# A gated delta-rule recurrence: side work of every engine in smaller pieces at other leaves, decay products on GpSimd, selector matmuls over row halves

## The chip, the core and the metric

The kernel is one launch on one core of a Trainium2 chip. The metric is the device time in microseconds of the whole launch, over several runs.

## The reference

An attention layer with a gated delta-rule state (2048 tokens, 16 heads of width 128) and after it a mixture-of-experts layer. The change is in the scan:

```python
def step(S, t):
    q_t, k_t, v_t, a_t, b_t = t
    y = jnp.einsum('bhvk,bhk->bhv', S, k_t)
    err = y - v_t
    S = a_t[..., None] * S - (b_t[..., None] * err)[..., None] * k_t[:, :, None, :]
    o = jnp.einsum('bhvk,bhk->bhv', S, q_t)
    return (S, o)
```

The outputs o are then normed over the head width, scaled by a gate and multiplied by Wo.

## The kernel before, in words

Three stages follow each other: projections and convolutions (tiles named A_), the recurrence (`recurrence`, tiles named B_), the experts (C_). The change is inside `recurrence`.

The recurrence takes 32 **chunks** of 64 tokens in order. A chunk has 16 **leaves** of 4 tokens, `j` from 0 to 15. A leaf is a chain over three engines. VectorE multiplies the coefficients with what came from the left (L1068), adds them up (L1071) and decays the result (L1073). TensorE transposes it into PSUM (L1576), ScalarE copies it to `WL`, and TensorE multiplies it with grams of keys and queries into `psM` (L1586 and L1588 for an even leaf, L1595 and L1603 for an odd one); the next leaf's L1068 reads that. `merge_of(j)` gives the size of the merge: even leaves merge 4 tokens, leaves 1, 5, 9, 13 merge 8, leaves 3 and 11 merge 16, leaf 7 merges 32. In the last two kinds the left side is first compacted into `WC` by ScalarE (`left_compact`). On the way the ends of the parts are scaled: by VectorE for even leaves (`scale_leaf`, L1031, and `scale_leaf_w`, L1036), by GpSimd for odd ones (`scale_right`, L822 and L830; `scale_left`, L840). After leaf 15 comes the **turn**: transposes of the whole W, the update of the state `ST` (L1541, L1018), and the next chunk's product of state with keys and queries (`contact`, L1449), copied by ScalarE.

All else is **side work**, and each engine has it written out by hand between leaves. For TensorE it is a table, `leaf_jobs(g, j)`, whose jobs are issued after leaf `j`'s merge: `qk` and `kk` (one row of queries or keys spread over all partitions by a selector, L1472), `own` and `gram` (grams, L1459 and L1495), `ktok` (transposed keys), `decay`, `oc`, `var`, `dev`, `rstd` (centering and norm of the outputs, L1517 is `var`), `wo` (output projection, L1533, in odd chunks only), `update`. Each job takes the next of five PSUM banks in turn and waits until the bank's last job has been read (`open_bank`). VectorE takes the banks: `y_terms` (L991) for `qk`, `row_pairs` for `kk`, `mask_own` and `mask_gram`, `decay_state` (L1012), `norm`. It also solves the leaves' small systems in eight steps (`leaf_solution`, L954) and makes the next chunk's decay products in three instructions (`decays`, L916, L919, L921). GpSimd's order is the list at the end of its block, where `past(g, j)` waits for VectorE to pass leaf `j`.

## Time and profile before

| what | value |
|---|---|
| runs | median 3173.81 us of 3 (3172.24 to 3183.9) |
| the profiled execution | 3174.62 us, span 3172.8 us |
| TensorE matmul, weight load | 2838.1 us (89%), 2012.0 us (63%) |
| VectorE | 2322.8 us (73%) |
| ScalarE | 1605.5 us (51%) |
| GpSimd | 1317.6 us (42%) |
| first and last L1068 of the recurrence | 642.2 us, 2781.9 us |

The two L1068 times bound the recurrence. The profile's slices show TensorE at 8 to 9 tenths and VectorE at 7 to 8 tenths over the whole of it. A matmul's record overlaps the next one's, so TensorE's busy time is more than its work.

### The profile page before, as it was taken

Reading aid. Unit: us, or ns where it says so; the run is one execution under the profiler, and the core shown is the slowest. Engines: PE = TensorE matmul, PEld = TensorE weight load, DVE = VectorE, ACT = ScalarE, POOL = GpSimd, SP = SyncE. Lnnn points to the kernel's source line nnn. Section 1 sums busy time; section 2 is a strip of 40 time slices with the busy share of each in tenths; the row PEclk is TensorE's granted clock in tenths of the full one; section 3 lists DMA queues with packets and bytes.
Section 4 is the critical chain, followed back from the end, with each engine's and each line's share of the span. In section 5 each row is a group of like instructions: output and inputs, shape, how many; then the busy total and the mean of one; then the engine's idle time right before and its main releaser. Section 6 shows DMA issues by size and latency. Waiting matters only on the chain. (4 is left out here: it accounts for less than half of the span.)

```text
span 3172.8 us, 48588 instructions
## 1 busy us (share of the span) xinstructions
PE 2838.1 (89%) x14144; PEld 2012.0 (63%) x14144; DVE 2322.8 (73%) x4837; ACT 1605.5 (51%) x3516; POOL 1317.6 (42%) x1574
## 2 busy tenths in 40 slices
PE   7999999678898898988989898898888989869999
PEld 3555555366676776666766676776767767645555
DVE  6777777578888778887787878788887788724332
ACT  6666666445555555554554555555555555421111
POOL 3666767624443444443443434444334444310000
PEclk9999999889999999999999999999999999979999
DMA  3655565631222322222323222322223222034220
GB/s 133 242 202 231 234 241 202 225 60 34 54 42 41 60 51 54 43 41 42 69 41 55 41 42 43 67 46 51 42 41 65 46 54 42 8 105 89 55 44 14
DMA packets 449884, 261.23 MB, mean 82 GB/s; under 512 B 402672, under 2 KB 414672, under 8 KB 447472
## 3 DMA queue, kind: packets, MB, share of 16 engines
q1 hardware_dynamic: 449664, 258.51, 31.5%
q8 instruction: 113, 1.85, 0.3%
q14 instruction: 107, 0.88, 0.1%
HBM read 153.42 MB, written 105.05 MB: 81 GB/s over the span
## 5 line engine op out<-in xcount | busy, mean ns | idle before, releaser
L265 DVE SCALAR_TENSOR_TENSOR A_acc<-A_psY,A_w,A_acc 128x410 f32<-128x410 f32 (+1 forms) x720 | 419.2, 637 | 151.6 <-ACT A_acc L334 151.6
L1155 ACT ACTIVATE B_WL<-B_psT 64x128 f32<-64x128 f32 (+3 forms) x480 | 148.6, 310 | 512.4 <-PE B_psT L1576 512.4
L840 POOL TENSOR_TENSOR B_WT<-B_WT,B_G 128x128 f32<-128x128 f32 (+2 forms) x224 | 183.0, 817 | 513.0 <-PE B_psT L1576 493.3
L405 PE MATMUL A_psY<-A_xT,A_w 128*128 128x413 f32 (+1 forms) x960 | 347.2, 510 | 9.1 <-PE A_psAG L411 7.7
L192 POOL TENSOR_TENSOR A_outs<-A_outs,A_acc 128x410 f32<-128x410 f32 (+1 forms) x240 | 229.7, 987 | 215.5 <-ACT A_outs L342 215.5
L1068 DVE TENSOR_TENSOR B_NC<-B_NC,B_psM 128x256 f32<-128x256 f32 x480 | 199.1, 415 | 143.9 <-PE B_psM L1603 101.8
L405 PEld LDWEIGHTS A_psY<-A_xT,A_w 128*128 128x128 f32 x960 | 180.2, 189 | 165.5 <-issue 164.2
L822 POOL TENSOR_TENSOR B_PQ<-B_PQ,B_G 128x256 f32<-128x256 f32 x128 | 125.8, 983 | 368.3 <-DVE B_WT L1036 368.3
L1071 DVE TENSOR_REDUCE B_W<-B_NC 128x64 f32<-128x320 f32 x512 | 248.7, 486 | 17.6
L1603 PE MATMUL B_psM<-B_BD,B_WL 128*128 128x128 f32 x1536 | 237.6, 296 | 12.6
L334 ACT ACTIVATE A_acc<-A_psY,A_w 128x410 f32<-128x410 f32 (+1 forms) x240 | 166.2, 692 | 162.9 <-PE A_psY L405 161.2
L1603 PEld LDWEIGHTS B_psM<-B_BD,B_WL 128*128 128x128 f32 x1536 | 195.9, 197 | 81.0 <-ACT B_WL L1155 80.3
L1155 ACT ACTIVATE B_PQ<-B_psM 128x64 f32<-128x64 f32 (+2 forms) x480 | 124.5, 259 | 220.8 <-DVE B_NC L1068 215.7
L411 PE MATMUL A_psAG<-A_xT,A_w 128*128 128x410 f32 (+1 forms) x640 | 233.1, 506 | 0.0
L830 POOL TENSOR_TENSOR B_PQ<-B_PQ,B_G 128x256 f32<-128x256 f32 (+1 forms) x192 | 174.9, 924 | 42.7 <-DVE B_WT L1036 42.7
L411 PEld LDWEIGHTS A_psAG<-A_xT,A_w 128*128 128x128 f32 x640 | 121.0, 189 | 99.6 <-issue 99.6
L954 DVE TENSOR_TENSOR B_NC<-B_NC,B_TMP 128x384 f32<-128x384 f32 (+1 forms) x192 | 164.5, 857 | 4.4
L1472 PE MATMUL B_ring<-B_QS,B_source 128*128 128x128 f32 (+1 forms) x896 | 158.7, 323 | 0.0
L793 POOL TENSOR_TENSOR B_SQ<-B_PQ,B_E 128x256 f32<-128x256 f32 x128 | 125.5, 981 | 71.1 <-DVE B_WT L1073 67.4
L1896 ACT ACTIVATE C_act_g<-C_psG 128x512 f32<-128x512 f32 (+1 forms) x56 | 33.4, 597 | 228.5 <-PE C_psU L1951 228.5
L1459 PE MATMUL B_ring<-B_KQ,B_KL 128*128 128x256 f32 x512 | 126.1, 390 | 25.6 <-DMA B_KQ<-scr 25.6
L1588 PE MATMUL B_psM<-B_OWN,B_WL 64*128 64x128 f32 x512 | 120.6, 315 | 20.0 <-ACT B_WL L1155 20.0
(197 smaller groups left out, 6703.5 us busy)
## 6 DMA issues: line engine op xcount, KB each, us to landing
B_KQ<-scr SPq DMA_DIRECT2D x96, 512.0 KB, 6.8
scr<-A_outs SPq DMA_DIRECT2D x48, 615.0 KB, 3.5
scr<-A_outag SPq DMA_DIRECT2D x32, 615.0 KB, 5.2
scr<-A_outs SPq DMA_DIRECT2D x48, 409.0 KB, 2.5
A_xc<-nbeta SPq DMA_DIRECT2D x16, 1024.0 KB, 5.9
B_A<-scr SPq DMA_DIRECT2D x32, 512.0 KB, 5.0
B_C<-scr SPq DMA_DIRECT2D x32, 512.0 KB, 5.9
B_G<-scr SPq DMA_DIRECT2D x32, 512.0 KB, 4.6
```

The costliest lines, as they stand in the source:

```text
L192: nc.gpsimd.tensor_tensor(o, o, acc[:, p, n % 2, 0:t1 - t0], ALU.mult).then_inc(silu[p].sem, 1)
L265: nc.vector.scalar_tensor_tensor(a, y, w[:, s, col:col + 1], a, ALU.mult, ALU.add)\
L334: nc.scalar.activation(acc[:, p, n % 2, 0:t1 - t0], psY[p][:, y0:y0 + t1 - t0], ACT.Identity, scale=w[:, s, col + HALO:col + HALO + 1], bi ...
L405: last = nc.tensor.matmul(psY[p][:, y0:y0 + HALO + t1 - t0], wp[:, p, kt, :], xT[:, kt, t0:t1 + HALO], start=kt == 0, stop=kt == KT - 1)
L411: last = nc.tensor.matmul(psAG[p][:, 0:t1 - t0], wp[:, A_ + p, kt, :], xT[:, kt, HALO + t0:HALO + t1], start=kt == 0, stop=kt == KT - 1)
L830: tt(x, x, gl.to_broadcast([128, H, n]), ALU.mult).then_inc(psc.sem, 1)
L840: tt(dst, dst, gr, ALU.mult).then_inc(wsc.sem, 1)
L954: tt(out, in0, in1, op).then_inc(ncs.sem, 1)
L1068: tt(eq[:, :, :, 1:5], eq[:, :, :, 1:5], left.unsqueeze(2).to_broadcast([128, H, R, R]), ALU.mult)\
L1071: nc.vector.tensor_reduce(W[:, :, lf], eq, AXIS.X, ALU.add).then_inc(ws.sem, 1)
L1155: copy = lambda out, in_: nc.scalar.activation(out, in_, ACT.Copy)
L1603: last = mm(psM[:, 512 * q + rs * i:512 * q + rs * (i + 1)], WL[0:rs, 128 * i:128 * (i + 1)], BD[0:rs, bank, col + rs * part:col + rs * (p ...
```

## The change

- The three decay products of the next chunk leave VectorE (`decays`) and become six products of one row each on GpSimd (`row_decays`), two behind leaf 2 and one each at leaves 6, 7 and twice at 9.
- The selector jobs `kk` and `qk` go over row halves: each of the two leaves of a pair has its own 64 rows and its own bank, and the matmuls alternate between the halves. `qk` is three jobs, not five, and `y_terms` reads two banks at a time. `update` alternates in the same way.
- A second table, `short_jobs`, puts TensorE's jobs between a leaf's transpose and its merge. Most jobs stand at other leaves; `wo` is cut in two halves.
- VectorE's side work moves with them; the eight solution steps are placed one by one, and the last of the next chunk's stands after the state update.
- In leaves 3, 7 and 11 VectorE writes its result straight into the compact array `WC`; ScalarE copies it from there to `WT` afterwards.
- In even leaves after the first, the product with `WL` comes before the one with the identity.
- Banks are given to the job by who had them longest ago, with two neighbouring ones for `kk` and `qk`. ScalarE's side work is regrouped.

```diff
+def short_jobs(g, j):
+    first, last, out, wo = g == 0, g + 1 == NCH, g > 0, g % 2 and g >= 3
+    jobs = {
+        2: [("own", 1, 1)],
+        3: [("ktok", 0)],
+        8: ([("own", 0, 0)] if not last else []),
+        10: [("gram", 5)],
+        14: ([("wo", 1)] if wo else []),
+    }
...
-            1: [("own", 1, 0), ("own", 1, 1)],
-            2: [("ktok", 0), ("gram", 1)] + (out and [("qk", 2)] or []),
-            3: out and [("qk", 3), ("qk", 4)],
-            4: [("kk", 1, 0), ("kk", 1, 1), ("gram", 4)],
-            5: out and [("oc", 0)],
-            6: out and [("oc", 1)],
-            7: out and [("oc_rest", 1)],
-            8: (g % 2 and [("ktok", 1)] or []) + ([] if last else [("own", 0, 0), ("own", 0, 1)]),
-            9: [("gram", 5), ("decay", 0), ("decay", 1)],
-            10: [] if last else [("kk", 0, 0), ("kk", 0, 1)],
-            11: out and [("var", 0)],
-            12: (out and [("dev", 0)] or []) + ([] if last else [("gram", 0)]) + (wo and [("wo", 0)] or []),
-            13: [("decay", 2), ("decay", 3)],
-            14: (wo and [("wo", 1)] or []) + (out and [("rstd", 0), ("rstd", 1)] or [])
-                + (not g % 2 and [("ktok", 1)] or [])}
-    return jobs.get(j) or []
+    jobs = {
+        -1: [("gram", 2), ("gram", 3)],
+        0: ([("qk", 0, 0), ("qk", 0, 1)] if out else []),
+        1: [("own", 1, 0)],
+        2: [("gram", 1)],
+        3: ([("qk", 1, 0), ("qk", 1, 1), ("qk", 2, 0), ("qk", 2, 1)] if out else []),
+        4: [("kk", 1, 0), ("kk", 1, 1), ("gram", 4)],
+        5: ([("oc", 0)] if out else []),
+        6: ([("oc", 1)] if out else []),
+        7: [("decay", 0)] + ([("oc_rest", 1)] if out else []),
+        8: ([("own", 0, 1)] if not last else []),
+        9: [("decay", 1)],
+        10: ([("kk", 0, 0), ("kk", 0, 1)] if not last else []) + ([("var", 0)] if out else []),
+        11: ([("wo", 0)] if wo else []),
+        12: ([("gram", 0)] if not last else []) + ([("dev", 0)] if out else []) + ([("wo_rest", 0)] if wo else []),
+        13: [("decay", 2), ("decay", 3)],
+        14: [("ktok", 1)] + ([("rstd", 0)] if out else []) + ([("wo_rest", 1)] if wo else []) + ([("rstd", 1)] if out else []),
+    }
+    return jobs.get(j, [])
...
-OUT_ROWS = [((0, 0, 2),), ((1, 1, 2),), ((2, 2, 2),), ((3, 3, 1), (0, 2, 1)), ((1, 3, 1), (0, 3, 1))]
+OUT_ROWS = [((0, 0, 2), (1, 1, 2)), ((2, 2, 2), (3, 3, 1), (0, 2, 1)), ((1, 3, 1), (0, 3, 1))]
+KEY_ROWS = ((0, 1, 3), (1, 2, 2), (2, 3, 1))
...
+            def row_decays(g, *parts):
+                a, e = by_leaf_row(A[:, g % 2]), E[:, g % 2]
+                products = ((RR_, a[:, 1], a[:, 2]), (B_, e[:, RR_], a[:, 3]), (F_ + 1, a[:, 0], a[:, 1]),
+                            (B_ + 1, a[:, 2], a[:, 3]), (F_ + 2, e[:, F_ + 1], a[:, 2]), (F_ + 3, e[:, F_ + 2], a[:, 3]))
+                for k in parts:
+                    row, x, y = products[k]
+                    if k == 0:
+                        loaded(pool, "A", g)
+                        wait(pool, nc0, 2 * g - 3, 5)
+                    else:
+                        wait(pool, dec, g, {1: 1, 4: 3, 5: 5}.get(k, 0))
+                    tt(e[:, row], x, y, ALU.mult).then_inc(dec.sem, 1)
...
+                if more:
+                    row_decays(g + 1, 0)
+                    row_decays(g + 1, 1)
...
                 past(g, 4)
                 scale_right(g, 5)
-                gates(3)
+                scale_left(g, 3)
                 past(g, 5)
-                queries(3)
+                if g:
+                    decayed_q(g - 1, 3)
+                if g >= 2:
+                    gate(g - 2, 3)
+                scale_right(g, 7, (0,))
                 scale_left(g, 5)
-                scale_right(g, 7, (0,))
+                scale_left(g, 7)
                 past(g, 6)
                 scale_right(g, 7, (1,))
+                if more:
+                    row_decays(g + 1, 2)
                 past(g, 7)
-                scale_left(g, 7)
+                if more:
+                    row_decays(g + 1, 3)
                 past(g, 8)
                 scale_right(g, 9)
                 past(g, 9)
+                if more:
+                    row_decays(g + 1, 4)
                 scale_left(g, 9)
+                if more:
+                    row_decays(g + 1, 5)
+                past(g, 11)
                 scale_right(g, 11)
-                past(g, 11)
-                scale_left(g, 11)
                 past(g, 12)
                 scale_right(g, 13)
-                past(g, 13)
+                scale_left(g, 11)
+                past(g, 14)
                 scale_left(g, 13)
...
-                wait(dve, awm, o, (4, 5, 3, 6, 6)[n])
-                ps = take_bank(dve, o + 1, "qk", n)
-                x = WX[:, 2 * n:2 * n + 2]
-                tt(x, ps[:].rearrange("p (n c) -> p n c", n=2), x, ALU.mult).then_inc(yv.sem, 1)
+                wait(dve, awm, o, (5, 6, 6)[n])
+                m = 4 if n < 2 else 2
+                ps = take_two_banks(dve, o + 1, "qk", n)[:, :, 0:m * HJ2]
+                x = WX[:, 4 * n:4 * n + m].rearrange("p k (l x) -> p l k x", l=2)
+                tt(x, ps.rearrange("p l (k x) -> p l k x", k=m), x, ALU.mult).then_inc(yv.sem, 1)
...
-                    tt(WT[:, j] if j % 2 else WR[:], W[:, :, lf], E[:, g % 2, B_:B_ + R, :, j].rearrange("p r h -> p h r"), ALU.mult).then_inc(wt.sem, 1)
+                    p, n, _ = merge_of(j)
+                    if j < JM and p >= 2:
+                        to = WC[:, 0:H * n].rearrange("p (h t) -> p h t", h=H)[:, :, n - R:n]
+                    else:
+                        to = WT[:, j] if j % 2 else WR[:]
+                    tt(to, W[:, :, lf], E[:, g % 2, B_:B_ + R, :, j].rearrange("p r h -> p h r"), ALU.mult).then_inc(wt.sem, 1)
...
+                    elif j == 8:
+                        if more:
+                            mask_own(g + 1, 0, 0)
                     elif j == 9:
                         if more:
-                            decays(g + 1, (1,))
-                            mask_own(g + 1, 0, 0)
                             mask_own(g + 1, 0, 1)
                     elif j == 10:
+                        decay_state(g, 0)
                         mask_gram(g, 5)
-                        decay_state(g, 0)
+                    elif j == 11:
                         decay_state(g, 1)
-                    elif j == 11 and more:
-                        row_pairs(nxt)
-                        leaf_solution(nxt, 1, 2)
-                    elif j == 12 and more:
-                        leaf_solution(nxt, 2, 4)
+                        if more:
+                            row_pairs(nxt)
+                            leaf_solution(nxt, 1)
+                    elif j == 12:
+                        if more:
+                            leaf_solution(nxt, 2)
...
-                        if p >= 2:
-                            wait(act, wt, g, j + 1)
-                            left_compact(g, j, (j,))
                         wait(act, tps, g, j + 1)
                         wait(act, mps, g, 2 * j)
                         w_ = 128 << max(p - 1, 0)
                         rows_ = 64 if p == 0 else 128
                         copy(WL[0:rows_, 0:w_], psT[0:rows_, 0:w_]).then_inc(wl.sem, 1)
+                        if p >= 2:
+                            wait(act, wt, g, j + 1)
+                            copy(WT[:, j], WC[:, 0:H * n].rearrange("p (h t) -> p h t", h=H)[:, :, n - R:n]).then_inc(wc.sem, 1)
                     if j == 13:
...
+            def row_scalars(g, kind, n):
+                if kind == "qk":
+                    rows, runs, width = QS[:, (g - 1) % 2].rearrange("p t h n -> p t (h n)"), OUT_ROWS[n], HJ2
+                else:
+                    rows, runs, width = KS[:], KEY_ROWS, HJ2 // 2
+                filled = [open_bank(pe, g, kind, n, leaf)[1] for leaf in range(2)]
+                if kind == "qk":
+                    wait(pe, qs, 2 * (g - 1) + 1, 1)
+                else:
+                    wait(pe, ks, 2 * g + (1 if n else 2), 1)
+                ps = two_banks(g, kind, n)
+                at = 0
+                for k, (r, t0, m) in enumerate(runs):
+                    for leaf in range(2):
+                        p = slice(64 * leaf, 64 * leaf + 64)
+                        c = R * leaf + r
+                        last = mm(ps[:, leaf, at * width:(at + m) * width].rearrange("p (t x) -> p t x", t=m),
+                                  source[p, c:c + 1].to_broadcast([64, 128]),
+                                  rows[p, R * leaf + t0:R * leaf + t0 + m], start=True, stop=True)
+                        if k == len(runs) - 1:
+                            last.then_inc(filled[leaf], 1)
...
+            def updates(g, half):
+                opened = [open_bank(pe, g, "update", 2 * half + r) for r in range(2)]
+                wait(pe, wtok, g, half + 1)
+                wait(pe, ktok, g, 2)
+                for m in range(4):
+                    i = 4 * half + m
+                    for r, (ps, filled) in enumerate(opened):
+                        p = slice(64 * r, 64 * r + 64)
+                        last = mm(ps[:, 128 * m:128 * (m + 1)], KTOK[p, i, :], WTOK[p, i, :], start=True, stop=True)
+                        if m == 3:
+                            last.then_inc(filled, 1)
...
                             wait(pe, ow, g, 2 if j < 8 else 4)
-                            wait(pe, psc0, g, pair_number(j) + 1)
-                            mm(psM[:, 0:2 * rs], ident[:], pair(g)[:, :, :, r0:r0 + n], start=True, stop=False)
-                            wait(pe, wl, g, j + 1)
-                            mm(psM[:, 0:2 * rs], WL[0:rs, 0:128], OWN[0:rs, j // 2, :, :, R:2 * R],
-                               start=False, stop=True).then_inc(mps.sem, 2)
+                            if j:
+                                wait(pe, wl, g, j + 1)
+                                mm(psM[:, 0:2 * rs], WL[0:rs, 0:128], OWN[0:rs, j // 2, :, :, R:2 * R], start=True, stop=False)
+                                wait(pe, psc0, g, pair_number(j) + 1)
+                                mm(psM[:, 0:2 * rs], ident[:], pair(g)[:, :, :, r0:r0 + n],```

VectorE's queue at leaves 8 to 10 of an even chunk (L1068 begins a leaf). Before:

```order
L1068 TENSOR_TENSOR B_NC<-B_NC,B_psM 128x16x4x4
L1071 TENSOR_REDUCE B_W<-B_NC 128x16x4
L1073 TENSOR_TENSOR B_WR<-B_W,B_E 128x64
L1045 TENSOR_TENSOR B_PQ<-B_PQ,B_psM 128x16x32
L1031 TENSOR_TENSOR B_PQ<-B_PQ,B_E 128x32x4
L1036 TENSOR_TENSOR B_WT<-B_WR,B_E 128x64
L916 TENSOR_TENSOR B_E<-B_A 128x3x256
L1068 TENSOR_TENSOR B_NC<-B_NC,B_psM 128x16x4x4
L1071 TENSOR_REDUCE B_W<-B_NC 128x16x4
L1073 TENSOR_TENSOR B_WT<-B_W,B_E 128x64
L919 TENSOR_TENSOR B_E<-B_E,B_A 128x2x256
L921 TENSOR_TENSOR B_E<-B_E,B_A 128x256
```

The same place in the changed kernel (L1137, L1140 and L1147 are the leaf's three, L1052 is `mask_own`):

```order
L1137 TENSOR_TENSOR B_NC<-B_NC,B_psM 128x16x4x4
L1140 TENSOR_REDUCE B_W<-B_NC 128x16x4
L1147 TENSOR_TENSOR B_WR<-B_W,B_E 128x64
L1114 TENSOR_TENSOR B_PQ<-B_PQ,B_psM 128x16x32
L1100 TENSOR_TENSOR B_PQ<-B_PQ,B_E 128x32x4
L1105 TENSOR_TENSOR B_WT<-B_WR,B_E 128x64
L1052 TENSOR_TENSOR B_OWN<-B_ring,B_causal 128x512
L1137 TENSOR_TENSOR B_NC<-B_NC,B_psM 128x16x4x4
L1140 TENSOR_REDUCE B_W<-B_NC 128x16x4
L1147 TENSOR_TENSOR B_WT<-B_W,B_E 128x64
L1052 TENSOR_TENSOR B_OWN<-B_ring,B_causal 128x512
```

The decays are gone, and one mask stands at each leaf where both stood behind leaf 9.

TensorE's queue from the merge of leaf 10 to the transposes of leaf 11, before:

```order
L1588 MATMUL B_psM<-B_OWN,B_WL 128x128
L1472 MATMUL B_ring<-B_KS,B_source 128x3x64 x2
L1472 MATMUL B_ring<-B_KS,B_source 128x2x64 x2
L1472 MATMUL B_ring<-B_KS,B_source 128x64 x2
L1576 MATMUL B_psT<-ident,B_WE 128x128 x2
```

And changed (L1590 is `gram`, L1733 and L1735 the merge, L1649 `kk`, L1612 `var`, L1723 the transposes):

```order
L1590 MATMUL B_ring<-B_KQ,B_KC 128x256 x2
L1733 MATMUL B_psM<-B_OWN,B_WL 128x128
L1735 MATMUL B_psM<-B_PQ,ident 128x128
L1649 MATMUL B_ring<-B_KS,B_source 128x192 x2
L1649 MATMUL B_ring<-B_KS,B_source 128x128 x2
L1649 MATMUL B_ring<-B_KS,B_source 128x64 x2
L1612 MATMUL B_ring<-B_SQ,B_avgcol 8x128 x8
L1723 MATMUL B_psT<-ident,B_WE 128x128 x2
```

`var` has moved from behind leaf 11 to behind leaf 10, and `gram` 5 in front of leaf 10's merge.

## Rows read from the trace of the kernel before

**Rows 1.** Windows, three chunks: engines' busy us, clock; even, odd, even.

```profile
core 0: us, PE busy (x) PEld busy (x) DVE busy (x) ACT busy (x) POOL busy (x), PEclk, DMA share, GB/s
1989.79:2054.51 64.72, 56.84 (x345) 43.45 (x344) 54.52 (x120) 36.12 (x85) 28.81 (x35) 1.00 0.28 49
2054.51:2123.29 68.78, 63.04 (x377) 49.62 (x376) 55.08 (x121) 36.40 (x86) 28.61 (x35) 1.00 0.26 49
1045.00:1112.00 67.00, 59.30 (x344) 45.55 (x343) 54.97 (x120) 36.05 (x85) 28.41 (x35) 0.95 0.27 48
```

**Rows 2.** Windows, even chunk: leaves 1, 2, 4, 6 and 7, 8 to 15.

```profile
1992.33:1995.22 2.89, 2.75 (x15) 2.30 (x16) 2.48 (x5) 1.86 (x9) 2.61 (x5) 1.00 0.03 6
1995.22:1998.49 3.27, 3.27 (x20) 2.74 (x19) 2.91 (x8) 1.97 (x5) 1.80 (x3) 1.00 0.01 5
2002.02:2005.27 3.25, 3.07 (x26) 2.74 (x24) 3.07 (x8) 1.86 (x7) 1.34 (x3) 1.00 0.00 0
2008.84:2018.71 9.87, 8.62 (x40) 5.14 (x39) 9.49 (x18) 4.59 (x10) 3.82 (x3) 1.00 0.36 60
2018.71:2022.47 3.76, 3.43 (x14) 1.99 (x13) 3.59 (x8) 2.19 (x4) 1.26 (x1) 1.00 0.00 0
2022.47:2026.72 4.25, 4.25 (x26) 3.40 (x24) 4.14 (x8) 1.09 (x3) 3.02 (x4) 1.00 0.00 0
2026.72:2030.39 3.67, 2.19 (x13) 1.60 (x12) 3.50 (x10) 3.32 (x8) 0.00 (x0) 1.00 0.00 0
2030.39:2033.65 3.26, 2.50 (x19) 1.97 (x18) 2.79 (x9) 1.77 (x7) 0.99 (x1) 1.00 0.00 0
2033.65:2037.24 3.59, 3.36 (x27) 2.45 (x26) 3.42 (x8) 1.40 (x4) 1.05 (x2) 1.00 0.02 5
2037.24:2040.38 3.14, 2.85 (x17) 2.16 (x18) 3.04 (x8) 1.73 (x4) 0.71 (x1) 1.00 0.00 0
2040.38:2044.00 3.62, 2.38 (x17) 1.72 (x15) 3.41 (x10) 1.32 (x4) 0.00 (x0) 1.00 0.01 2
2044.00:2054.51 10.51, 9.13 (x84) 8.36 (x82) 6.03 (x12) 6.58 (x10) 6.83 (x10) 1.00 0.86 152
```

**Rows 3.** Windows, odd chunk: leaf 13, and leaf 15 with the turn.

```profile
2101.99:2107.46 5.47, 5.33 (x27) 4.57 (x28) 3.03 (x8) 1.58 (x4) 0.46 (x1) 1.00 0.00 0
...
2111.10:2123.29 12.19, 11.89 (x99) 11.07 (x98) 6.54 (x13) 6.10 (x9) 6.83 (x10) 1.00 0.79 144
```

**Rows 4.** Groups of instructions, VectorE, whole launch: busy us, mean ns.

```profile
L991 DVE TENSOR_TENSOR B_WX<-B_ring,B_WX 128x512 f32<-128x512 f32 x160 | 107.3, 687 | 8.1 <-PE B_ring L1472 6.4
L916 DVE TENSOR_TENSOR B_E<-B_A 128x768 f32<-128x768 f32 x32 | 50.3, 1573 | 1.7 <-ACT B_E L1155 1.5 <-issue 0.2
L919 DVE TENSOR_TENSOR B_E<-B_E,B_A 128x512 f32<-128x512 f32 x32 | 34.7, 1085 | 0.3
L921 DVE TENSOR_TENSOR B_E<-B_E,B_A 128x256 f32<-128x256 f32 x32 | 24.5, 766 | 1.1
```

**Rows 5.** Timeline, TensorE: start us, us, line, shape, passes.

```profile
1976.74 3.72 PE L1533 MATMUL B_ring<-B_wo,B_OG 128*128 128x256 f32 x16
...
2002.27 1.95 PE L1472 MATMUL B_ring<-B_QS,B_source 128*128 128x128 f32 x16
...
2029.50 1.75 PE L1472 MATMUL B_ring<-B_KS,B_source 128*128 128x192 f32 x12
...
2033.99 1.91 PE L1517 MATMUL B_ring<-B_SQ,B_avgcol 128*8 128x128 f32 x16
...
2047.23 2.79 PE L1541 MATMUL B_ring<-B_WTOK,B_KTOK 64*128 64x128 f32 x32 [0.30 <-issue]
```

**Rows 6.** Timeline: a solution step beside GpSimd's work and without it.

```profile
2010.89 1.54 POOL L830 TENSOR_TENSOR B_PQ<-B_PQ,B_G 128x512 f32<-128x512 f32 x1 [1.33 <-DVE B_WT L1036]
2011.49 1.42 DVE L954 TENSOR_TENSOR B_NC<-B_X,B_NC 128x256 f32<-128x256 f32 x1
...
2035.67 0.61 DVE L954 TENSOR_TENSOR B_NC<-B_X,B_NC 128x256 f32<-128x256 f32 x1
```

390 lines of the change are left out of this document (223 added, 167 removed).

## The prediction, made blind

> **What bounds the kernel now.** I read the busy slices first: the recurrence fills two thirds of the span, with no engine full and the same pattern throughout, and the change is in it alone. So the next view is the table of windows, one chunk of 64 tokens each [rows 1]: an even chunk takes 64.72 us, an odd one 68.78. In the even one VectorE is busy 54.52 us and TensorE 56.84, and the reader should see that neither share is a bound by itself: TensorE's record overlaps itself, and each leaf of four tokens is a chain (VectorE solves the leaf, TensorE transposes it, ScalarE copies it, TensorE merges it, VectorE takes the result). A leaf's time is the longer of two things: that chain, with the side work in front of it on TensorE, or the work in VectorE's own queue. The windows by leaf [rows 2] tell which. Leaves 6 and 7 together: VectorE 9.49 of 9.87 us; leaf 8: 3.59 of 3.76; leaf 9: 4.14 of 4.25; leaf 10: 3.50 of 3.67; leaf 14 of the even chunk: 3.41 of 3.62. Those are VectorE's. Leaf 1 (2.48 of 2.89) and leaf 13 of the odd chunk (3.03 of 5.47) [rows 3] are TensorE's. At the chunk's turn (leaf 15) it is a serial chain: 6.03 of 10.51.
>
> **What the operations cost.** The three decay products cost VectorE 1573, 1085 and 766 ns, 3.42 us a chunk [rows 4]. They go to GpSimd as six products of 256 elements. VectorE's y terms are five of 687 ns [rows 4]; three with the same elements in all keep most of that, a 512-element one standing every 0.62 us, so I take 0.15 us off. On TensorE an fp32 matmul is two passes. 16 passes of 128 columns over all 128 rows take 1.91 to 1.95 us, 0.12 each; the state update's 32 passes of the same width on 64 rows, first one half of the rows, then the other, take 2.79 us, 0.09 each [rows 5]. So a row half starts before the other has ended. For alternating halves the bounds are 0.12 (no gain) and 0.06 (full overlap); I take 0.065, as the row shows overlap already where the halves only meet at a boundary. The selector job of the keys, 12 passes in 1.75 us [rows 5], becomes about 0.9, twice a chunk. The queries have 16 passes of 128 columns (1.95) and 12 twice as wide, about 4.4 us together, and go to 2.3.
>
> **Leaf by leaf**, in us a chunk, before from [rows 2, 3]:
> Leaf 1: the query job in front of its transpose shrinks from 1.7 to 0.9 us, so the transpose goes when VectorE is done (1.3 instead of 1.7 us into the leaf): −0.4.
> Leaf 2: half of the own-gram job now stands between transpose and merge, and the mask waits for it: +0.25.
> Leaf 4: it takes over 1.7 us of y terms where it had 1.3, and was at 3.07 of 3.25: with 0.2 us of gaps 3.85, +0.6.
> Leaves 6 and 7: GpSimd's scaling of the right part is moved out of leaf 6 and now follows the scaling of the left part in leaf 7. In leaf 6 it stood in VectorE's way: the solution step that begins at 2011.49 takes 1.42 us, and the same step takes 0.61 us at 2035.67 when GpSimd is still [rows 6]. The 0.8 us saved in leaf 6 is paid in leaf 7: −0.1.
> Leaf 8: loses the first decay product (1.57), gains a mask of 0.68 us, but waits for a job between transpose and merge behind decay 0 and the centered rest: 3.5, −0.25.
> Leaf 9: loses 1.85 us of decays and a mask; the chain of 3.0 us is left: −1.25.
> Leaf 10: loses one state decay (0.68) but has a gram between transpose and merge: 3.35, −0.3.
> Leaf 11: TensorE now has key selectors (0.9) and the variance job (16 passes, 1.91 [rows 5]) in front of the transpose, 2.8 us into the leaf instead of 1.6, and it was TensorE's leaf: +1.1.
> These eight sum to −0.35, in every chunk.
> Even chunks: leaf 12 without the variance job and with one solution step less, −0.65; leaf 13 has a solution step of 0.86 more on VectorE, +0.8; leaf 14 one less and its mask first, −0.55; leaf 15 as before. Together −0.4, so −0.75.
> Odd chunks: the output projection, 16 passes of 256 columns in 3.72 us [rows 5] in front of leaf 13, is halved there: 5.47 becomes 4.4, −1.1. Leaf 12 gets the first half, 0. Leaf 14 gets a half between transpose and merge, +0.4. The turn has 3.1 us instead of 3.7 in front of its transposes, −0.6. Together −1.3, so −1.65.
> Leaves 0, 3 and 5 I cost at nothing: the compaction that goes from leaf 3 is replaced by GpSimd's two decays beside it, and in leaf 5 ScalarE's copies of the key rows end when they did. If that cover is gone each is worth 0.3 us, either way. The last solution step after the state update lies under VectorE's wait for the contact copies (10.51 − 6.03 us idle in the turn [rows 2]).
>
> **What moves past what.** The decays wait in GpSimd's queue for nothing that is late: A is loaded a chunk ahead, and the first of them stands behind leaf 2. Behind them in that queue are the scalings for leaves 5, 9 and 11; each has over 1 us to spare, by GpSimd's 28.81 busy of 64.72 us [rows 1], which becomes about 34. ScalarE's leaf diagonals wait for the sixth product, which I place half a microsecond into leaf 10, and they start later. No DMA is added, and SP's queue sees the same semaphores. Key and query selectors need two neighbouring PSUM banks; the key job of leaf 4 waits 0.3 us for a y term's banks, under VectorE's 3.85 us. In even leaves after the first, the WL product now goes ahead of the identity product, so two matmuls follow the copy instead of one (about +0.2), where VectorE's scaling was late anyway: nothing.
>
> **The sum.** 16 × 0.75 + 15 × 1.65 = 37 us. The profiled execution took 3174.6 us (span 3172.8), the median of the runs is 3173.8, so the two agree: **3137 us**. Each leaf's term may be off by 0.3 us, which over a chunk is about 1 us, or 31 us in all: the forecast's own range is 3105 to 3168.
>
> **A rule on GpSimd.** The solution steps in [rows 6] show VectorE and GpSimd taking turns: one step of 0.61 us became 1.42. The Trainium skill (GPSIMD Engine Reference, section 8, Key points) says that GpSimd shares its SBUF interfaces with VectorE where VectorE's instruction has two SBUF inputs; by that rule, and the trace agrees, the decays could slow VectorE although they left its queue. That is the slower rival below.
> **A rule on row halves.** The pass of 64 rows costs less in [rows 5], with the update's two halves one behind the other. The Trainium skill (TensorEngine Tiling, Key Properties) says that a change of tiling mode drains TensorE. The change adds such switches round the selector jobs of leaves 3, 4 and 10; if each cost a pass and more, the gain of the halves would be gone.
>
> **The rivals.**
> *VectorE bounds all of it.* Then a chunk loses all of the 3.57 us that leave its queue: 31 × 3.57 = 111, **3063 us**. For it: 54.5 us busy in either kind of chunk [rows 1]. Against it: in odd leaf 13 and in leaf 11 it waits.
> *Slower by the shared port.* The six products on GpSimd each can hold a two-input step of VectorE by 0.8 us as in [rows 6]. My sum is −1.2 us a chunk, so it turns at 1.5 such holds; with three of the six it is +1.2 × 31, **3211 us**. For it: products 3 to 6 are queued behind leaves 6 to 9, the first of them behind two scalings that already collide. Against it: VectorE reads PSUM in most of its work there.
> *The halves don't overlap, or switching eats it.* Leaf 1 gives nothing, leaf 11 costs 0.75 more: +1.15 a chunk, **3173 us**, no change.
> *The clock.* A chunk in which the granted clock was 0.95 took 67.00 us against 64.72 [rows 1]. That window holds both levels, 2.4 and 1.2 GHz, while the other two chunks there stay at 1.00, and its work was the even chunk's. For it: TensorE gets less to do. If half of the chunks had that: +2.3 × 16, again **3173 us**.
>
> **How the numbers follow.** My forecast 0.47, VectorE's bound 0.20, no overlap 0.12, the port 0.11, the clock 0.10. A difference of 0.5% (16 us) is about what a measurement here can tell. Faster than 3158: 0.38 of the forecast's share, 0.20, and 0.06 of the milder halves of the others, 0.64. Within 0.5%: 0.08, and 0.10 from overlap and clock, 0.18. Slower: 0.18, of it 0.10 the port, the rest the bad ends of clock and overlap. The range reaches from the second case (3063, rounded down) to just short of the port's price: 3060 to 3200.
>
> **What would show it.** Right: leaf 9 near 3.0 us, leaf 4 near 3.9, leaf 11 near 4.3, odd leaf 13 near 4.4; selector passes starting in pairs; VectorE busy about 51 us a chunk. Wrong: solution steps of 1.4 us in more places than before (port), selector passes still 0.11 us apart (overlap), clock windows under 1.00 in most chunks, or leaf 11 near 3.3 (then I have misread what stands before its transpose).

## The result, and the profile after

The changed kernel took **3100.56 us** in the median (3098.51 to 3104.37 over 4 runs), the kernel before 3174.42 (3172.24 to 3183.9): ratio 0.9763, 95% interval [0.9747, 0.9779], so 74 us faster. Forecast were 3137 us, 37 us faster. The direction held, and the time lies in the whole range of 3060 to 3200 us, but 5 us outside the forecast's own of 3105 to 3168: the gain is twice the one that the sum gave. The profiled execution of the changed kernel took 3104.37 us (span 3102.6, mean granted clock 0.976; before 0.977).

Windows of one even and one odd chunk, as in [rows 1]:

```profile
core 0: us, PE busy (x) PEld busy (x) DVE busy (x) ACT busy (x) POOL busy (x), PEclk, DMA share, GB/s
1940.50:2003.46 62.96, 53.29 (x345) 38.96 (x344) 51.88 (x116) 36.26 (x85) 30.53 (x41) 1.00 0.28 52
2003.46:2069.57 66.11, 59.72 (x377) 44.65 (x376) 52.65 (x117) 36.56 (x86) 30.54 (x41) 1.00 0.26 50
```

The even chunk lost 1.76 us and the odd one 2.67. 16 × 1.76 + 15 × 2.67 = 68 us. In the two profiled executions the recurrence is 72 us shorter, and the other 4 are chunks with a lower clock. They are more now, but each costs less: of the 15 even chunks from 2 to 30, 9 have a stretch under 1.00 and take 0.7 to 2.0 us longer for it; before, 5 had one, for 2.3 to 2.5 us, and one odd chunk, for 3.3. VectorE is busy 51.88 us instead of 54.52, GpSimd 30.53 instead of 28.81.

The even chunk by leaf: leaves 1, 4 to 13 and 15 (leaf 7 begins at 1963.45). A leaf is counted from VectorE's first multiplication in it (L1137) to that of the next.

```profile
1943.05:1945.57 2.52, 2.02 (x15) 1.39 (x12) 2.31 (x5) 1.60 (x4) 2.52 (x5) 1.00 0.40 79
1952.56:1956.32 3.76, 3.31 (x33) 2.62 (x33) 3.59 (x9) 2.96 (x7) 1.36 (x2) 1.00 0.00 0
1956.32:1959.43 3.11, 2.97 (x24) 2.37 (x21) 2.54 (x8) 1.54 (x6) 1.80 (x3) 1.00 0.00 0
1959.43:1963.45 4.02, 3.57 (x13) 1.88 (x12) 3.85 (x11) 1.51 (x4) 1.30 (x2) 1.00 0.84 169
1963.45:1969.46 6.01, 5.79 (x32) 3.78 (x31) 5.80 (x9) 3.10 (x6) 3.06 (x3) 1.00 0.42 66
1969.46:1972.94 3.48, 3.45 (x14) 1.98 (x14) 2.89 (x7) 1.80 (x3) 1.74 (x3) 1.00 0.00 0
1972.94:1975.46 2.52, 2.02 (x11) 1.34 (x10) 1.78 (x4) 2.00 (x4) 1.20 (x2) 1.00 0.00 0
1975.46:1978.94 3.48, 2.80 (x17) 1.87 (x16) 3.09 (x8) 2.58 (x8) 0.91 (x2) 1.00 0.00 0
1978.94:1983.25 4.31, 4.27 (x38) 3.32 (x39) 3.41 (x8) 1.91 (x8) 1.25 (x2) 1.00 0.00 0
1983.25:1986.21 2.96, 1.62 (x10) 1.14 (x9) 2.45 (x7) 1.66 (x6) 0.72 (x1) 1.00 0.00 0
1986.21:1990.02 3.81, 3.23 (x20) 2.29 (x18) 3.71 (x8) 2.19 (x5) 0.77 (x2) 1.00 0.00 0
1993.03:2003.46 10.43, 8.87 (x89) 8.19 (x87) 6.84 (x14) 6.58 (x10) 7.17 (x10) 1.00 0.87 152
```

The odd chunk's leaf 13, and leaf 15 with the turn:

```profile
2049.86:2053.93 4.07, 3.76 (x20) 2.92 (x19) 3.79 (x8) 2.30 (x6) 0.10 (x1) 1.00 0.01 4
2058.16:2069.57 11.41, 10.47 (x97) 9.74 (x96) 7.47 (x14) 6.58 (x10) 7.19 (x10) 1.00 0.79 144
```

Against [rows 2] and [rows 3] the reader should see four leaves that carry the gain: leaf 9 went from 4.25 to 2.52 us with VectorE busy only 1.78 of it, and 2.52 is the length of leaf 1 too; odd leaf 13 from 5.47 to 4.07; leaf 5, whose row was not shown before, from 3.57 (it lay between 2005.27 and 2008.84 in [rows 2]) to 3.11; leaf 1 from 2.89 to 2.52. Leaf 11 gave back 1.05 (3.26 to 4.31), TensorE busy 4.27 of it.

GpSimd's decay products, which answer to [rows 4], and the selector jobs of leaves 3 and 4 in TensorE's timeline, which answer to [rows 5]:

```profile
L830 POOL TENSOR_TENSOR B_E<-B_E,B_A 128x256 f32<-128x256 f32 x93 | 80.2, 863 | 53.0 <-DVE B_WT L1147 50.6
...
L830 POOL TENSOR_TENSOR B_E<-B_A 128x256 f32<-128x256 f32 x93 | 69.7, 762 | 2.4 <-DVE B_WR L1147 2.4
```

```profile
1952.90 1.59 PE L1649 MATMUL B_ring<-B_QS,B_source 64*128 64x256 f32 x20
...
1955.98 0.99 PE L1649 MATMUL B_ring<-B_KS,B_source 64*128 64x192 f32 x12
```

The six products cost GpSimd 0.76 to 0.86 us each in the mean. The y terms (L1061), now two of 1217 ns and one of 680 in a chunk, take VectorE 3.11 us instead of 3.43. The 12 key passes take 0.99 us instead of 1.75, the last 20 query passes 1.59; in both jobs each pass of one row half starts 5 to 7 ns behind one of the other half.

Leaf 7's solution steps beside GpSimd, as in [rows 6]:

```profile
1966.40 1.16 POOL L899 TENSOR_TENSOR B_WT<-B_WT,B_G 128x512 f32<-128x512 f32 x1 [5.67 <-ACT B_WT L1244]
1966.57 1.47 DVE L1023 TENSOR_TENSOR B_TMP<-B_X,B_NC 128x384 f32<-128x384 f32 x1
1967.52 1.44 POOL L887 TENSOR_TENSOR B_PQ<-B_PQ,B_G 128x512 f32<-128x512 f32 x1
...
1968.07 1.36 DVE L1023 TENSOR_TENSOR B_NC<-B_NC,B_TMP 128x384 f32<-128x384 f32 x1
...
1968.91 1.00 POOL L830 TENSOR_TENSOR B_E<-B_A 128x256 f32<-128x256 f32 x1
```

Two steps of leaf 7, the first beside the scaling of the left part (L899), the second beside that of the right part (L887), take 1.47 and 1.36 us. The second one takes 0.6 us when GpSimd is still (in the last experiment). In leaf 6, where one step took 1.42 before, no solution step is held now. Two of leaf 3's rows show a held instruction that is no solution step, VectorE's decay of the leaf's result:

```profile
1949.93 0.65 POOL L830 TENSOR_TENSOR B_E<-B_A 128x256 f32<-128x256 f32 x1
1950.02 0.69 DVE L1147 TENSOR_TENSOR B_WE<-B_W,B_E 128x64 f32<-128x64 f32 x1
```

It takes 0.27 us in the kernel before and 0.68 now, both medians over the chunks, because the first of GpSimd's products starts just ahead of it; in e2, where that product is gone, it takes 0.27 again. Leaves 2 and 14, without a row here, take 3.48 and 3.01 us in the median.

### The profile page after: what moved, and what is told of

Its sections match the earlier page's. It is cut to its first block and busy times, and to the rows that moved or that the text cites. A ratio compares the mean times of both kernels' runs of the same rounds, so it can differ in the third digit from the quotient of the medians.

```text
span 3102.6 us, 48417 instructions
## 1 busy us (share of the span) xinstructions
PE 2732.2 (88%) x14144; PEld 1863.5 (60%) x14144; DVE 2239.8 (72%) x4680; ACT 1610.3 (52%) x3516; POOL 1377.8 (44%) x1760
## 5 line engine op out<-in xcount | busy, mean ns | idle before, releaser
L1244 ACT ACTIVATE B_PQ<-B_psM 128x64 f32<-128x64 f32 (+2 forms) x480 | 125.2, 261 | 441.2 <-DVE B_NC L1137 440.9
L1137 DVE TENSOR_TENSOR B_NC<-B_NC,B_psM 128x256 f32<-128x256 f32 x480 | 200.8, 418 | 182.5 <-PE B_psM L1756 92.8
L899 POOL TENSOR_TENSOR B_WT<-B_WT,B_G 128x128 f32<-128x128 f32 (+2 forms) x224 | 143.4, 640 | 371.2 <-ACT B_WT L1244 184.3
L1244 ACT ACTIVATE B_WL<-B_psT 64x128 f32<-64x128 f32 (+3 forms) x480 | 148.5, 309 | 265.6 <-PE B_psT L1723 265.4
L1140 DVE TENSOR_REDUCE B_W<-B_NC 128x64 f32<-128x320 f32 x512 | 248.7, 486 | 17.6
L879 POOL TENSOR_TENSOR B_PQ<-B_PQ,B_G 128x256 f32<-128x256 f32 x128 | 89.4, 699 | 345.5 <-DVE B_WT L1105 345.5
L1756 PE MATMUL B_psM<-B_BD,B_WL 128*128 128x128 f32 x1536 | 228.2, 288 | 12.4 <-ACT B_WL L1244 4.6
L887 POOL TENSOR_TENSOR B_PQ<-B_PQ,B_G 128x256 f32<-128x256 f32 (+1 forms) x192 | 159.6, 845 | 128.3 <-DVE B_WE L1147 127.6
L1023 DVE TENSOR_TENSOR B_NC<-B_NC,B_TMP 128x384 f32<-128x384 f32 (+1 forms) x192 | 184.7, 962 | 3.3
L1568 PE MATMUL B_ring<-B_KQ,B_KL 128*128 128x256 f32 x512 | 139.5, 396 | 25.4 <-DMA B_KQ<-scr 25.3
L1733 PE MATMUL B_psM<-B_OWN,B_WL 64*128 64x128 f32 x448 | 106.7, 319 | 51.7 <-ACT B_WL L1244 51.7
L1723 PE MATMUL B_psT<-ident,B_WR 128*64 128x128 f32 x256 | 75.7, 296 | 86.3 <-DVE B_WR L1147 85.1
```

The costliest lines, as they stand in the source:

```text
L887: tt(x, x, gl.to_broadcast([128, H, n]), ALU.mult).then_inc(psc.sem, 1)
L1023: tt(out, in0, in1, op).then_inc(ncs.sem, 1)
L1137: tt(eq[:, :, :, 1:5], eq[:, :, :, 1:5], left.unsqueeze(2).to_broadcast([128, H, R, R]), ALU.mult)\
L1140: nc.vector.tensor_reduce(W[:, :, lf], eq, AXIS.X, ALU.add).then_inc(ws.sem, 1)
L1244: copy = lambda out, in_: nc.scalar.activation(out, in_, ACT.Copy)
L1756: last = mm(psM[:, 512 * q + rs * i:512 * q + rs * (i + 1)], WL[0:rs, 128 * i:128 * (i + 1)], BD[0:rs, bank, col + rs * part:col + rs * (p ...
```

## The experiments

Each kernel is the changed one with one edit, but for e5, which starts from the kernel before, and e6, e9, e10 and e12, which join several edits. Each ratio is to the kernel before, timed on the same chip. Leaf times without a row are medians over the chunks, taken from the same start times.

### Row halves in turn

```diff
-                for k, (r, t0, m) in enumerate(runs):
-                    for leaf in range(2):
+                for leaf in range(2):
+                    at = 0
+                    for k, (r, t0, m) in enumerate(runs):
```

> The changed kernel, with the selector passes of one row half all ahead of those of the other, so that the halves can overlap only where they meet. Theory (row halves that alternate overlap in full, and leaf 5's 0.46 us came from the key job in front of its transpose): leaf 1 +0.37, leaf 4 +0.3, leaf 5 +0.46, leaf 11 +0.6 us, together 1.7 us a chunk, 53 us, so about 3153 us (ratio 0.993), and the 12 key passes take about 1.4 us instead of 0.8. Rival A (leaf 5 is shorter because ScalarE's copies moved): leaf 5 stays at 3.11, 3139 us. Rival B (halves in turn overlap half as well, as the state update's 0.09 us a pass suggests): 3127 us. Rival C (the decays made the gain alone): 3100 us.

Measured: 3127.32 us, ratio 0.9839 [0.9822, 0.9857], 0.8% slower than the changed kernel. TensorE's timeline of the key job, and the window of leaf 5 behind it:

```profile
1974.98 1.41 PE L1650 MATMUL B_ring<-B_KS,B_source 64*128 64x192 f32 x12
```

```profile
1975.09:1978.62 3.53, 3.39 (x24) 2.98 (x25) 2.55 (x7) 1.92 (x6) 2.20 (x3) 1.00 0.00 0
```

Leaf 5 rose from 3.11 to 3.53 us, leaf 11 from 4.31 to 4.74, leaf 4 by 0.30; leaf 1 stayed at 2.52, and the step behind leaf 5 fell by 0.18. So the length of the key job sets leaf 5, and rival A's figure of 3.11 us falls. But the path is not the one through the transpose that the theory named. VectorE's row pairs wait for ScalarE's copies of the key rows:

```profile
1977.25 0.42 DVE L1006 TENSOR_TENSOR B_NC<-B_ring,B_A 128x128 f32<-128x128 f32 x1 [0.91 <-ACT B_X L1244]
```

In the changed kernel this wait is 0.50 us. In 24 of the 26 chunks from 4 to 29 the next leaf's first multiplication then follows VectorE's queue at once, without a wait for TensorE's merge. A longer key job thus reaches the end of leaf 5 through the copies.

The total is that of rival B. In the trace the first pass of the second half starts 0.434 us behind the job's first pass and before the fourth pass of the first half: TensorE overlaps the halves in part even when they are issued in turn, so the order is worth 0.42 us a key job (1.14 us from the first start to the last, 0.72 alternating). Leaf 1's job, 8 passes of 256 columns, starts its passes within 0.81 us alternating and 0.76 in turn; there the order is worth nothing.

### The decays back on VectorE

```diff
-            if more:
-                row_decays(g + 1, 0)
...
+                    elif j == 8:
                         if more:
+                            decays(g + 1, (0,))
                             mask_own(g + 1, 0, 0)
                     elif j == 9:
                         if more:
+                            decays(g + 1, (1,))
                             mask_own(g + 1, 0, 1)
```

> The changed kernel, with the decays on VectorE again: the first product in leaf 8, the other two in leaf 9, none on GpSimd. Theory (leaf 9 fell to 2.52 us because VectorE's queue was its only bound): leaf 8 becomes VectorE's with 2.89 + 1.57 = 4.5 to 4.6 us (+1.1), leaf 9 becomes 1.78 + 1.85 = 3.7 us (+1.2), nothing elsewhere: +2.3 us a chunk, 71 us, 3172 us (ratio 0.999), so the move of the decays alone carries as much as the whole change. Rival A (leaf 9 fell because half of the own-gram job left the front of its transpose): leaf 9 stays under 3.3, total 3155 us or less. Rival B (GpSimd's products cost something through held VectorE steps): leaf 3 and leaf 7 get shorter by up to 0.8 us each, and the total is under 3150 us.

Measured: 3246.55 us, ratio **1.0215** [1.0191, 1.0239]: slower than the kernel before. The windows of leaves 9 to 11, and the variance job in leaf 11:

```profile
2069.74:2073.42 3.68, 1.81 (x11) 1.34 (x11) 3.54 (x8) 1.43 (x3) 0.86 (x2) 1.00 0.00 0
2073.42:2077.39 3.97, 2.68 (x11) 1.78 (x11) 3.08 (x10) 3.63 (x9) 0.00 (x0) 0.84 0.00 0
2077.39:2084.33 6.94, 6.90 (x38) 4.89 (x39) 3.46 (x8) 1.45 (x6) 1.24 (x2) 0.60 0.00 0
```

```profile
2078.97 3.58 PE L1609 MATMUL B_ring<-B_SQ,B_avgcol 128*8 128x128 f32 x16
```

Leaves 8 and 9 did what was expected (4.35 and 3.68 us, together 2.03 more than in the changed kernel). Leaf 3 fell from 3.51 to 3.29 us, since no product of GpSimd now meets its result: 0.22 us a chunk is what the moved decays cost VectorE there, a small part of rival B. Leaves 10 and 11 were expected to stay and took 3.97 and 6.94: the granted clock is 0.84 and 0.60 there, a mixture of 1.2 and 2.4 GHz, and the 16 variance passes take 3.58 us instead of 1.91 [rows 5]. In every chunk from 2 to 30 leaf 11 took 5.5 to 7.0 us. Before it fell, TensorE had been busy 1.81 of leaf 9's 3.68 us. No theory on record had this; it is the mechanism of the prediction's clock rival, set off by leaving the decays where they were. The run e10 below tests it.

### The decays alone, on the kernel before

```diff
-                        decays(g + 1, (0,))
...
-                            decays(g + 1, (1,))
...
+                if g + 1 < NCH:
+                    row_decays(g + 1, 2, 3)
```

> The kernel before, with the decays alone moved to GpSimd (the change's six products, at its places in GpSimd's queue). Theory: leaf 8 falls from 3.76 to about 3.3 us (then what stands between its transpose and its merge bounds it), leaf 9 from 4.25 to 3.1 (both halves of the own-gram job, 1.5 us, still stand in front of its transpose): -1.6 us a chunk, 50 us, 3125 us (ratio 0.984). Rival A (VectorE's queue is the bound throughout): all 3.42 us of the decays go, 3069 us. Rival B (the six products hold VectorE's steps as the scalings do, 0.8 us each, three of them): +2.4 us a chunk against -1.6, 3200 us. Rival C (the run with decays on VectorE in the changed kernel lost 146 us through TensorE's clock alone, the decays themselves are worth little): under 1% faster, above 3145 us.

Measured: 3146.17 us, ratio 0.9888 [0.9863, 0.9913]. Windows of leaves 7, 8 and 9 and of leaf 15:

```profile
1992.36:1997.92 5.56, 4.55 (x26) 2.96 (x25) 5.36 (x9) 2.72 (x6) 3.08 (x3) 1.00 0.00 0
1997.92:2001.22 3.30, 2.59 (x11) 1.38 (x9) 2.20 (x6) 2.10 (x4) 1.12 (x2) 1.00 0.00 0
2001.22:2004.11 2.89, 2.75 (x15) 2.30 (x16) 2.48 (x6) 1.29 (x4) 1.57 (x3) 1.00 0.00 0
2021.48:2034.19 12.71, 11.63 (x85) 10.70 (x84) 6.04 (x13) 6.69 (x10) 6.78 (x10) 0.75 0.86 157
```

Leaf 8 fell to 3.30 us as expected and leaf 9 to 2.89, 0.2 more. But leaf 7 rose from 5.20 to 5.56, as a product beside its last solution step holds it for 0.96 us instead of 0.61 (a small form of rival B), and in 7 of the 14 even chunks from 4 to 30 the turn took more than 11.8 us; the one shown took 12.71 at a clock of 0.75, against 10.5 in all 14 before. The decays by themselves are worth 1.1%, half of the change.

### The decays back once more, with TensorE fed

The kernel of e6 (below) with the decays as in e2. Against e2 half of the variance job stands in leaf 10, the first state decay is a leaf earlier, and leaf 9 has one more job for TensorE:

```diff
-        9: [("decay", 1)],
+        9: [("decay", 1), ("gram", 5)],
```

> The kernel of e6_var_split_banks with the decays on VectorE again, as in e2_decays_back. There leaf 10 and leaf 11 lost 0.9 and 2.4 us, and the granted clock was 0.84 and 0.60 in them. Here TensorE has gram 5 in leaf 9 and half of the variance job earlier. Theory (the loss in leaves 10 and 11 was TensorE's clock, which fell after a stretch in which TensorE had little to do, 1.81 us busy of 3.68 in leaf 9): with more of TensorE's work there the clock holds, only leaf 8 +0.9 and leaf 9 +1.8 us remain, 84 us on 3067, about 3150 us (ratio 0.991). Rival A (the clock falls here too, as leaf 9 is longer still): leaves 10 and 11 together above 8.5 us, 3200 us or more. Rival B (leaves 10 and 11 waited in e2 for what depends on the decays, ScalarE's leaf diagonals, whatever the clock): the same loss at a clock of 1.00.

Measured: 3154.03 us, ratio 0.9929 [0.9913, 0.9944]. Leaves 9, 10 and 11:

```profile
2009.91:2014.20 4.29, 2.68 (x15) 2.00 (x15) 4.15 (x9) 1.91 (x4) 0.86 (x2) 1.00 0.00 0
2014.20:2017.62 3.42, 2.14 (x15) 1.45 (x15) 2.38 (x8) 2.59 (x8) 0.00 (x0) 1.00 0.00 0
2017.62:2021.15 3.53, 3.53 (x31) 2.72 (x32) 3.33 (x9) 1.91 (x8) 1.24 (x2) 1.00 0.00 0
```

The clock stays at 1.00 in these leaves, in all but 2 of the chunks from 2 to 30 (in leaves 12 to 15 it falls in 12 of the 15 even ones); leaf 10 takes 3.42 and leaf 11 3.53 us, although leaf 9 is longer than in e2 and ScalarE's leaf diagonals still wait for the decays. So the clock made e2's loss in leaves 10 and 11, and rival B falls. Which of the moved jobs kept the clock up isn't separated: leaf 9 has more for TensorE, and leaf 11 less. That e5's turn has the same cause is read from its row alone.

### The variance job in two halves

```diff
-        10: ([("kk", 0, 0), ("kk", 0, 1)] if not last else []) + ([("var", 0)] if out else []),
+        9: [("decay", 1)] + ([("var", 0)] if out else []),
+        10: ([("kk", 0, 0), ("kk", 0, 1)] if not last else []) + ([("var_rest", 0)] if out else []),
```

> The changed kernel, with the variance job cut in two: 8 of its 16 passes in front of leaf 10's transpose, 8 behind the key selectors in front of leaf 11's. Theory (leaf 11 is TensorE's, 1.6 us plus what stands in front of its transpose; leaf 10 has room, 3.09 us of VectorE in 3.48): leaf 11 falls from 4.31 to about 3.5 (VectorE is busy 3.41 of it), leaf 10 stays: -0.8 us a chunk, 25 us, 3076 us (ratio 0.969). Rival A (leaf 10 has no room on TensorE, its gram stands between transpose and merge): leaf 10 +0.5, 3091 us. Rival B (leaf 11 is bound by VectorE's row pairs, not by TensorE): no change, 3100 us.

Measured: 3111.33 us, ratio 0.9793 [0.9775, 0.981]. Leaf 11 fell to 3.53 us as expected, but leaf 10 rose from 3.48 to 4.63, where the theory had it stay and rival A 0.5 more, and odd leaf 13 from 4.07 to 4.45. The timeline of leaf 10, gram 5 on TensorE (L1590) and VectorE's mask of it (L1043):

```profile
1982.45 0.68 DVE L1081 TENSOR_TENSOR B_ST<-B_ST,B_ring 128x512 f32<-128x512 f32 x1
...
1983.18 1.13 PE L1590 MATMUL B_ring<-B_KQ,B_KC 128*128 128x256 f32 x4 [0.81 <-DVE B_ST L1081]
...
1984.35 0.69 DVE L1043 TENSOR_TENSOR B_BD<-B_ring,B_E 128x512 f32<-128x512 f32 x1 [1.22 <-PE B_ring L1590]
```

Gram 5 waits for VectorE's state decay (L1081), which reads the bank that it needs: with one more job in between, the five banks came round to the one of decay 0. The next kernel repairs that:

```diff
     8: ([("own", 0, 0)] if not last else []),
-        10: [("gram", 5)],
+        10: ([("var", 0)] if out else []),
...
-        9: [("decay", 1)],
+        9: [("decay", 1), ("gram", 5)],
...
                             mask_own(g + 1, 0, 1)
+                        decay_state(g, 0)
                     elif j == 10:
-                        decay_state(g, 0)
```

> The changed kernel, with the variance job cut in two as in e3_var_split, but gram 5 in leaf 9 ahead of it, the first half between transpose and merge of leaf 10, and the first state decay a leaf earlier, so that the bank of decay 0 is free when it is wanted. Theory (e3 lost 1.15 us in leaf 10 only because gram 5 then waited for the bank that the first state decay reads until 5.09 us behind leaf 9's start): leaf 10 stays at 3.5, leaf 11 falls from 4.31 to 3.5 us: -0.8 us a chunk, 25 us, 3076 us (ratio 0.969). Rival A (TensorE's total work in leaves 9 to 11 sets their time, wherever it stands): no change, 3100 us. Rival B (less work in front of leaf 11 lets the clock fall): leaf 10 or 11 above 4.5 us, 3110 us or more.

Measured: 3073.44 us, ratio **0.9653** [0.9637, 0.967], 1.1% faster than the changed kernel. Leaves 10 and 11:

```profile
1957.47:1960.91 3.44, 3.44 (x25) 2.48 (x24) 2.41 (x8) 2.54 (x8) 0.91 (x2) 1.00 0.00 0
1960.91:1964.44 3.53, 3.52 (x31) 2.71 (x32) 3.33 (x9) 1.91 (x8) 1.25 (x2) 1.00 0.00 0
```

Leaf 10 takes 3.44, leaf 11 3.53 us instead of 4.31, and odd leaf 13 4.07 again. Both windows are full of TensorE, but the first multiplication behind leaf 11 now follows VectorE's queue without a wait, so VectorE is as much its bound. The theory held, and with it the prediction's reading of leaf 11 in the changed kernel.

### GpSimd's order in leaves 6 and 7

```diff
                 scale_left(g, 5)
-                scale_left(g, 7)
                 past(g, 6)
                 scale_right(g, 7, (1,))
...
                 past(g, 7)
+                scale_left(g, 7)
```

> The changed kernel, with GpSimd's second scaling of the right part of merge 7 ahead of the scaling of the left part again, as before the change. Theory of the prediction (a solution step of VectorE that meets a GpSimd product takes 1.4 us instead of 0.6, and the change only moved that from leaf 6 to leaf 7): leaf 6 +0.8, leaf 7 -0.8 us, total 3100 us within 6. Rival A (both held steps of leaf 7 go, one comes back in leaf 6): -0.8 us a chunk, 3076 us. Rival B (the holds do not depend on the order): leaves 6 and 7 as they are.

Measured: 3123.48 us, ratio 0.9826 [0.981, 0.9843], slower than the changed kernel by 0.6%, where all theories had it equal or better. Leaf 6 rose from 4.03 to 5.19, leaf 7 fell from 6.01 to 5.63 only. The timeline of leaf 6:

```profile
1975.94 1.55 POOL L887 TENSOR_TENSOR B_PQ<-B_PQ,B_G 128x512 f32<-128x512 f32 x1 [0.92 <-DVE B_WT L1105]
...
1976.54 1.42 DVE L1023 TENSOR_TENSOR B_NC<-B_X,B_NC 128x256 f32<-128x256 f32 x1
...
1977.45 0.90 POOL L830 TENSOR_TENSOR B_E<-B_A 128x256 f32<-128x256 f32 x1
...
1977.80 1.26 DVE L1023 TENSOR_TENSOR B_NC<-B_NC,B_TMP 128x384 f32<-128x384 f32 x1
```

The step at 1976.54 is held by the scaling (L887), and the next one by the third product (L830), 1.26 us instead of 0.87. In leaf 7 the fourth product holds the last step again, 0.96 us. The products cost VectorE something wherever they meet a step that reads two SBUF tiles.

```diff
-                scale_left(g, 7)
                 past(g, 6)
+                wait(pool, mps, g, 14)
                 scale_right(g, 7, (1,))
+                scale_left(g, 7)
```

> The changed kernel, with GpSimd's second scaling of the right part of merge 7 released by merge 6, so that it runs while VectorE reads PSUM at the start of leaf 7 and not beside the solution steps of its end. Theory (only a VectorE step with both inputs in SBUF is held, so one of leaf 7's two held steps of 1.4 us becomes 0.6): leaf 7 falls from 6.01 to 5.2 us, leaf 6 stays: 25 us, 3075 us (ratio 0.969). Rival A (the scaling is held instead, or holds the decay result and the next steps just as long): no change, 3100 us. Rival B (as in e4_right7_early, the first row decay then meets a step): -0.4 us, 3088 us.

Measured: 3087.23 us, ratio 0.9707 [0.9691, 0.9723]. Leaf 7 takes 5.61 us:

```profile
1957.29 1.97 POOL L830 TENSOR_TENSOR B_E<-B_A 128x256 f32<-128x256 f32 x2
...
1957.82 0.96 DVE L1024 TENSOR_TENSOR B_NC<-B_NC,B_TMP 128x384 f32<-128x384 f32 x1
```

The scaling of the right part now holds nothing, but the products moved up into its place and the last step takes 0.96: rival B. Leaf 7's 0.4 us make 12 of the 18 us gained. Of the rest the traces show 3: as many even chunks have a lower clock as in the changed kernel, 9 of 15, but they cost less.

### The output projection whole

```diff
-        11: ([("wo", 0)] if wo else []),
-        12: ... + ([("wo_rest", 0)] if wo else []),
+        12: ... + ([("wo", 0), ("wo_rest", 0)] if wo else []),
```

(and the second job likewise, whole in leaf 14)

> The changed kernel, with the two output projection jobs of odd chunks whole again, behind leaf 12 and behind leaf 14. Theory (the time of odd leaf 13 is what stands in front of its transpose plus 1.6 us): odd leaf 13 +1.4, odd leaf 12 -0.6, odd leaf 14 -0.6, odd leaf 15 +0.8: +1.0 us in each of 15 chunks, 15 us, 3116 us (ratio 0.981). Rival (TensorE's total work counts, wherever it stands): 3100 us within 4.

Measured: 3127.7 us, ratio 0.9832 [0.9816, 0.9849]; odd leaf 13:

```profile
2065.26:2071.07 5.81, 5.50 (x28) 4.44 (x27) 3.81 (x9) 2.32 (x6) 0.77 (x2) 1.00 0.01 3
```

Odd leaf 13 rose by 1.7 us, leaf 15 with the turn by 1.7, leaf 14 fell by 1.2 and leaf 12 by 0.65: together 1.5 us a chunk where the theory had 1.0, most of the difference in the turn, which was put at 0.8. The rival falls. The halved jobs are worth 0.7%.

### Compaction by ScalarE

```diff
-                    if j < JM and p >= 2:
-                        to = WC[:, 0:H * n].rearrange("p (h t) -> p h t", h=H)[:, :, n - R:n]
-                    else:
-                        to = WT[:, j] if j % 2 else WR[:]
+                    to = WT[:, j] if j % 2 else WR[:]
```

> The changed kernel, with the last leaf result of merges 3, 7 and 11 written where the others are and compacted by ScalarE in front of the transposes, as before the change. Theory (the prediction gave this part nothing, but in leaf 3, 7 and 11 the transposes wait for the result): leaf 3 and leaf 7 are close to VectorE's or TensorE's queue; leaf 3 +0.4 us, leaf 7 0 (VectorE is busy 5.81 of 6.01), leaf 11 0 (its transposes wait for TensorE's jobs until 2.6 us into the leaf): +0.4 us a chunk, 12 us, 3113 us. Rival A (the copy lies in all three chains): +1.2 us, 3138 us. Rival B (costs nothing): 3100 us.

Measured: 3114.36 us, ratio 0.9802 [0.9787, 0.9817]. In leaf 3 the copy stands in the chain, between VectorE's result and the transposes:

```profile
1958.45 0.26 ACT L1241 ACTIVATE B_WE<-B_WT 128x64 f32<-128x64 f32 x1 [0.16 <-DVE B_WT L1144]
...
1958.80 0.41 PE L1720 MATMUL B_psT<-ident,B_WE 128*128 128x128 f32 x2 [1.22 <-ACT B_WE L1241]
```

Leaf 3 rose from 3.51 to 3.81 and leaf 8 from 3.48 to 3.71 us; leaves 7 and 11 stayed. The theory held in size, 0.4% for this part, but not in place: it had nothing for leaf 8, and why that leaf rose wasn't followed up. In leaf 3 this saving of 0.30 us and the 0.22 that GpSimd's products cost (e2) nearly cancel, as the prediction had it.

### Both improvements together

e6 and e7 in one kernel, with the third product moved behind `past(g, 7)`:

> The changed kernel with the parts of e6_var_split_banks and e7_right7_behind_merge6 together, and the third of GpSimd's six products moved from leaf 7 into leaf 8, next to the fourth, since in e7 it met the last solution step of leaf 7 (0.96 us instead of 0.61). Theory (the parts act in different leaves, so they add): leaf 7 5.25, leaf 10 3.44, leaf 11 3.53 us; e6 gave 0.9653, e7 0.9707 against 0.9763 of the change, the moved product another 0.3 us a chunk: ratio 0.957, 3037 to 3045 us. Rival (the product then holds VectorE in leaf 8, whose slack is 0.6 us, by more than that): ratio 0.960.

Measured: 3054.91 us, ratio 0.9619 [0.9605, 0.9632]. Leaf by leaf the two parts add: leaves 7, 10 and 11 take 5.61, 3.44 and 3.52 us. The ratios of e6 and e7 would add to 0.9597, a little outside the interval; whether more than noise is in that isn't known. The moved product gave nothing of the 0.003 expected of it: leaf 7's own result releases it, so it still ran inside leaf 7. Then behind the scaling for leaf 9:

```diff
                 past(g, 7)
-                if more:
-                    row_decays(g + 1, 2, 3)
                 past(g, 8)
                 scale_right(g, 9)
+                if more:
+                    row_decays(g + 1, 2, 3)
```

> The kernel of e9_both, with GpSimd's third and fourth product behind its scaling for leaf 9: in e9_both they still ran in leaf 7 (8.11 and 9.10 us behind leaf 6's start), since leaf 7's own result releases them, and the last solution step took 0.96 us. Theory (a product beside a solution step costs VectorE 0.35 us, beside the leaf's multiplication, which reads PSUM, nothing): leaf 7 falls from 5.61 to 5.25 us, leaves 8 and 9 stay: 11 us, ratio 0.9585 (about 3043 us). Rival A (the scaling for leaf 9's merge is now late behind two products): leaf 9 +0.3, no gain, ratio 0.962. Rival B (leaf 8's own steps are held instead, its slack is 0.6 us): ratio between the two.

Measured: 3053.72 us, ratio **0.9609** [0.9596, 0.9623]. Leaf 7 is 5.25 us as expected, but leaf 8 took 3.87 instead of 3.52. Its timeline, VectorE's last solution step and TensorE's jobs:

```profile
1934.58 0.60 DVE L1022 TENSOR_TENSOR B_NC<-B_NC,B_TMP 128x384 f32<-128x384 f32 x1
...
1936.65 0.59 PE L1707 MATMUL B_ring<-B_WX,B_center 128*128 128x256 f32 x2
...
1937.08 0.27 PE L1733 MATMUL B_psT<-ident,B_WR 128*64 128x128 f32 x1
```

The step takes 0.60 us, but the transpose of leaf 8 (L1733) waits for the centered rest (L1705 to L1707), whose last part starts at 1936.65. So leaves 7 and 8 together take 9.12 us as in the run before. What was late next is TensorE's queue, no rival on record. The two last versions are the same within their intervals; the last is 3.9% faster than the kernel before and 1.6% faster than the changed one.

## Why the prediction was right in direction and half in size

The mechanism held: a leaf is as long as its chain with the jobs in front of it, or as VectorE's queue. Two terms of the sum failed in size, those of leaf 9 and of leaf 5.

- **Leaf 9: "loses 1.85 us of decays and a mask; the chain of 3.0 us is left".** This term failed most: −1.73 us, forecast −1.25. With the decays gone and the own-gram job whole in front of its transpose (e5) the leaf took 2.89; I had read 3.0 and had not counted that the change moves half of that job into leaf 8. Its 0.37 us make the leaf 2.52, the shortest that any leaf takes here: the transpose now goes 1.30 us into the leaf, when VectorE's result is there, and not at 1.72 behind the job.
- **Leaf 5: "I cost at nothing … ScalarE's copies of the key rows end when they did".** It gained 0.46 us. The copies did end nearly when they did: VectorE's row pairs, which wait for them, begin 1.78 us into the leaf before and 1.74 after. But before the change they were not the bound. The leaf ended with a wait for TensorE's merge:

```profile
2008.84 0.42 DVE L1068 TENSOR_TENSOR B_NC<-B_NC,B_psM 128x256 f32<-128x256 f32 x1 [0.27 <-PE B_psM L1603]
```

Its transpose stood behind the key job, 2.40 us into the leaf, and goes at 1.54 now. The merge is then ready early, and VectorE's queue behind the copies bounds the leaf, so only part of the 0.86 us is gained; e1 shows that the key job still sets it by that path (3.53 us with a longer job). The same mistake as in leaf 9: the job ahead of the transpose was not followed into this leaf, although leaf 1 and leaf 11 were worked out by just that.
- **Leaf 8** −0.28 (forecast −0.25), **leaf 1** −0.37 (−0.4), **leaf 2** +0.21 (+0.25), **leaf 4** +0.51 (+0.6), **leaf 11** +1.05 (+1.1), **leaf 10** −0.19 (−0.3): right. The e6 run shows that leaf 11's term had the right cause. **Leaf 3** stayed at its length (3.53 and 3.51) by the two opposite effects that the prediction names.
- **Leaves 6 and 7, "the 0.8 us saved in leaf 6 is paid in leaf 7"**: right in kind, 9.87 to 10.03 us, +0.16 instead of −0.1.
- So the eight common terms came to −0.64 instead of −0.35 and leaf 5 adds −0.46, −1.10 us a chunk: 0.75 more than forecast, times 31 is 23 of the 37 us that were missing. The misses of leaves 9 and 5 alone, 0.94 us a chunk, would be 29; leaves 6 and 7 took 8 of them back.
- **Even chunks**: leaf 12 −0.63 (−0.65), leaf 13 +0.67 (+0.8), leaf 14 −0.61 (−0.55), leaf 15 −0.08 (0): right; 0.25 too little, 4 us. **Odd chunks**: leaf 13 −1.40 (−1.1), leaf 14 +0.6 (+0.4), turn −0.78 (−0.6), leaf 12 0 (0): 0.3 too little, 4 us. Of the remaining 6 us, 4 are the clock; the rest is the difference between the profiled executions and the medians.
- **Row halves**: 0.065 us a pass was taken; 12 passes in 0.99 us are 0.08, with the switches at both ends in it, 20 passes in 1.59 us the same. The queries, put at 2.3 us, take 2.8 in their two stretches (1.19 and 1.59). The rival "no overlap" falls. The Trainium skill (TensorEngine Tiling, Key Properties) says that a change of mode drains TensorE; in the trace the first pass behind each such change starts 0.20 us after the last one before it, where passes of one kind follow in 0.11, and the next one comes late once more by 0.10 (0.32 us instead of 0.22 for passes of 256 columns). So a change costs about 0.2 us, with the trace on the page's side, and that is too little to undo the gain: from the first key pass to the first of the gram behind it, in front of leaf 5's transpose, it takes 0.92 us instead of 1.59.
- **GpSimd's products**: the rival "slower by the shared port" had the mechanism right, and the price and the number of holds wrong. A product of 256 elements beside a solution step costs VectorE 0.35 us (0.96 against 0.61), not the 0.8 of a 512-element scaling. In the changed kernel one product holds something, the first: leaf 3's result takes 0.68 us instead of 0.27, for 0.22 us a chunk (e2), about 7 in all. The third one starts at 1968.91, when the last step is under way, and adds next to nothing to leaf 7; in e4, e5 and e7 one holds that step. The moved scalings gave something back that the prediction did not count: before, a solution step of leaf 12 met one as well (1.28 us in the median, 0.68 more than undisturbed), and in even chunks one of leaf 13, and neither does now. GpSimd's busy time came to 30.53, not 34.
- **VectorE bounds all of it** (3063 us) did not happen: leaf 9's VectorE is busy 1.78 of 2.52 us.
- **The clock**: the rival came true in number and not in price. It had half of the chunks at a mixed clock for 2.3 us each; 9 of the 15 even chunks from 2 to 30 are, and none of the odd ones from 3, but for 0.7 to 2.0 us each, 11 us in all, and the kernel before paid 15 for the same. The runs also show that the parts of the change need each other: without the moved decays the other parts make the kernel 2.1% slower, since TensorE's work, bundled into leaf 11 behind a thin leaf 9, then runs at the lower clock (e10 supports this, without showing which job does it). Moving the decays is worth 1.1% on the kernel before, and 4.5% with the other parts in place (1.0215 against 0.9763), most of it the clock. A sum of parts, each costed on the kernel before, could not show that.

What stays open is the worth of two parts. The worth of 64-row passes against 128-row ones was measured only through their order (0.8%). A kernel with the old full-row selectors and everything else changed wasn't tried, and the part of the moved scalings isn't measured by itself.

## What to carry to other kernels

When a step is a chain through several engines, follow every job in front of the waiting instruction into the next step, and through every engine that reads it, not only in those where that engine looks like the bound: both terms that failed here were a job that shrank or moved one place ahead. Work that leaves a queue should be placed by the clock as well, since a thin stretch on TensorE followed by a bundle of its jobs can cost the bundle nearly double (3.58 us for the variance passes of 1.91, in e2). And of work moved to GpSimd, ask which VectorE instruction with two SBUF inputs it will run beside. Beside a PSUM reader it cost nothing here: the first multiplication of leaf 7 in the last run took 0.43 us beside the scaling of the right part, and 0.42 without it.

## What the hardware showed that was not expected

- Passes on the two row halves overlap even when all of one half are issued ahead of the other's: the first of the second half starts 0.434 us into the job, ahead of three of the six before it (e1).
- Decay products put back on VectorE in leaves 8 and 9 took the granted clock of the next two from 1.00 to 0.84 and 0.60 (e2), and leaf 15 with the turn, 10.51 us before, took 12.71 at a clock of 0.75 in e5, with less work on VectorE.
- A VectorE instruction of 64 elements took 0.69 us instead of 0.27 beside a GpSimd product of 256 (leaf 3 of the changed kernel).
- The five banks go round in order of use: one more job between two others made TensorE's gram wait 0.81 us for a bank, and VectorE's mask, which had no wait in the changed kernel, 1.22 us (e3, L1043).
